# Dense attention: the target-row addition moved from VectorE to GpSimd for four of every five source tiles

## The reference, cut to what matters

```python
e = leaky_relu(es[src] + ed[dst], 0.2)       # es, ed: one score per node and head
m = segment_max(e, dst, num_segments=n)
w = exp(e - m[dst])
den = segment_sum(w, dst, num_segments=n)
out = segment_sum(h[src] * (w / den[dst])[:, :, None], dst, num_segments=n)
```

## Time and profile before

| | |
|---|---|
| median of three runs | 7711.75 us (7710.52 to 7715.44) |
| profiled execution, its own time | 7714.48 us |
| its span, first to last instruction | 7712.8 us |
| VectorE busy in the span | 4335.9 us, 56% |
| TensorE busy | 5320.6 us, 69% |
| ScalarE busy | 2284.1 us, 30% |
| GpSimd busy | 1473.0 us, 19% |
| mean granted TensorE clock | 0.85 |

### The profile page before, as it was taken

The page is one execution under the profiler, slowest core; times in us unless marked ns, Lnnn a source line. Parts: engine busy times, 40 slices in busy tenths (PEclk is TensorE's granted clock), DMA queues, the critical chain, the costliest instruction groups (busy, mean ns, idle before and its releaser), DMA issues. The chain is left out here.

```text
span 7712.8 us, 81237 instructions
## 1 busy us (share of the span) xinstructions
PE 5320.6 (69%) x21589; PEld 3583.0 (46%) x21589; DVE 4335.9 (56%) x6661; ACT 2284.1 (30%) x3965; POOL 1473.0 (19%) x1601
## 2 busy tenths in 40 slices
PE   0223788877888599898597639639925777666976
PEld 0011344443444366677475418538823333335754
DVE  6100599946999322232684460301138999987857
ACT  0000211122111233222363103212215777754611
POOL 0775166602666000001000000030020000000000
PEclk9655899998999699999798869769967888877978
DMA  0011433354334100033230002145523444432200
GB/s 25 26 38 52 188 100 108 99 168 168 110 100 97 43 8 8 10 96 113 87 112 21 1 13 69 36 151 186 182 67 120 155 156 155 149 92 92 91 12 17
DMA packets 379927, 679.26 MB, mean 88 GB/s; under 512 B 94754, under 2 KB 306907, under 8 KB 372156
## 3 DMA queue, kind: packets, MB, share of 16 engines
q1 hardware_dynamic: 304364, 519.11, 20.5%
q0 software_dynamic: 75344, 157.40, 7.9%
HBM read 503.61 MB, written 172.62 MB: 88 GB/s over the span
## 5 line engine op out<-in xcount | busy, mean ns | idle before, releaser
L598 POOL DMA_INDIRECT sum_rows_in<-rel_table,rel_row x880 | 847.8, 963 | 455.1 <-issue 234.5
L622 DVE TENSOR_SCALAR sum_hot_cell<-x_nodes 128x1500 bf16<-128x1500 f16 (+1 forms) x880 | 892.4, 1014 | 1.0 <-issue 0.9
L676 PE MATMUL ps<-sum_hot_cell,sum_hot_src 128*128 128x500 bf16 x2640 | 766.1, 394 | 165.2 <-issue 84.5
L1504 PE MATMUL ps<-att_ring,acc 125*65 125x500 f32 x1000 | 606.8, 693 | 303.8 <-DVE att_ring L1326 303.5
L545 PE MATMUL ps<-rel_diag,rel_xt 128*128 128x512 f32 x800 | 436.1, 693 | 407.7 <-issue 175.7
L681 PE MATMUL ps<-sum_rows_in,sum_hot 128*128 128x256 f32 x1760 | 592.0, 415 | 65.3 <-issue 63.7
L778 PE MATMUL ps<-aux,sum_wide 125*125 125x256 f32 x2500 | 579.1, 387 | 54.5 <-ACT sum_wide L727 54.5
L1512 PE MATMUL ps<-acc,att_ring 125*125 125x257 f32 x2500 | 561.2, 387 | 73.4 <-DVE att_ring L1326 46.0
L942 POOL COPY aux<-prep_xin 128x256 f32 x75 | 30.1, 415 | 2987.4 <-DVE prep_xin L977 2987.4
L1442 ACT ACTIVATE att_ring<-att_ring,att_src 125x625 f32<-125x625 f32 x750 | 545.4, 804 | 126.3 <-DVE att_ring L1307 126.2
L1307 DVE TENSOR_TENSOR att_ring<-att_ring,att_rows 125x3125 f32<-125x3125 f32 (+1 forms) x162 | 512.4, 3169 | 93.8 <-ACT att_ring L1401 92.6
(11 more groups left out here) (432 smaller groups left out, 7532.4 us busy)
## 6 DMA issues: line engine op xcount, KB each, us to landing
att_cell<-cells SPq DMA_DIRECT2D x150, 781.2 KB, 4.7
att_masks<-masks SPq DMA_DIRECT2D x150, 762.9 KB
rel_table<-rel_stage SPq DMA_DIRECT2D x50, 2048.0 KB
ffn_w<-in_L_ffn_W SPq DMA_DIRECT2D x64, 1024.0 KB, 7.3
sum_cell<-cells SPq DMA_DIRECT2D x250, 156.2 KB, 2.2
masks<-sum_stage POOLq DMA_DIRECT2D x25, 762.9 KB, 11.7
sum_rows_in<-rel_table,rel_row POOLq DMA_INDIRECT x880
cells<-x_nodes SPq DMA_DIRECT2D x5, 2031.2 KB
```

The lines of the kernel that those rows point to most:

```text
L598: pool.indirect_dma_start(rows_in[:, b, u, :], None, table, bass.IndirectOffsetOnAxis(rows[:, k:k + 1], 0)).then_inc(gathered[b], 16)
L622: dve.tensor_scalar(hot_cell[:, b, u, :], K.columns[:, :, 0:CW], K.cell[:, k], None, ALU.is_equal).then_inc(s_hot, 1)
L676: pe.matmul(K.ps[:, bass.ds(side * 4 + j, 1), 0:BW].rearrange("p a n -> p (a n)"), hot_src[:, b, u, :], hot_cell[:, b, u, j * BW:(j + 1) * ...
L1504: pe.matmul(K.ps[0:W, side, 0:BAND], node_rows[s][0:NPT, h, :], ring[0:NPT, b % RB, v, 0:BAND], start=s == 0, stop=s == NT - 1).then_inc(s ...
```

## The change

`lower(b)` no longer adds the row to five tiles. VectorE makes only the first tile of a batch (`own_tiles`; all five in batch 0), and it makes it whole, without ScalarE's Relu: one scalar_tensor_tensor of 125x625, max(both + 0.8 s, low row), where `both` is the sum of the two rows. GpSimd adds the low row to the other four tiles, in two instructions of 125x1250 each, and once per group, from the second on, makes `both` (125x625). Two counters are new: `s_low` (GpSimd's pairs, for which the exponentials of tiles 2 to 5 wait) and `s_both`. ScalarE's bend(b) has four Relus, none in batch 0. To make room in memory `top` and `low` move into the tile `K.gate`, which is idle in these stages, and the tiles of the routed expert layer are freed after it.

```diff
--- before.py
+++ after.py
@@ -1218,12 +1218,14 @@
         s_row, s_rowed, s_max, s_top, s_wide, s_rows = (ph.sem(n) for n in ("row", "rowed", "max", "top", "wide", "rows"))
         s_z, s_w, s_e, s_p, s_mm, s_out = (ph.sem(n) for n in ("z", "w", "e", "p", "mm", "out"))
         s_diag, step, s_bias = ph.sem("diag"), ph.sem("step"), ph.sem("bias")
+        s_low, s_both = ph.sem("low"), ph.sem("both")
         ring = ph.sb("ring", [P, RB, UN, GW])
         warm = ph.sb("warm", [P, 1])
         if across:
             s_turned, s_back, turned = ph.sem("turned"), ph.sem("back"), ph.sb("turned", [P, GW])
-        rows = ph.sb("rows", [P, 2, 2, GW])
-        top, low = ph.sb("top", [P, heads, NT]), ph.sb("low", [P, heads, NT])
+        rows, both = ph.sb("rows", [P, 2, 2, GW]), ph.sb("both", [P, GW])
+        idle = K.gate[:, :, :].rearrange("p t e -> p (t e)")
+        top, low = (idle[:, j * 4 * NT:(j * 4 + heads) * NT].rearrange("p (h t) -> p h t", h=heads) for j in range(2))
         src8, src2, dst8 = (ph.sb(n, [P, NT, 4]) for n in ("src8", "src2", "dst8"))
         s_parts = ph.sem("parts")
         bias, total = ph.sb("bias", [P, D]), ph.sb("total", [P, NT, heads])
@@ -1244,6 +1246,18 @@
             return q == g and g * UN < loops
 
         diags = [sum(looped(c) for c in range(b + 1)) for b in range(NB)]
+
+        def own_tiles(b):
+
+            return UN if b == 0 else 1
+
+        def by_vector(batches):
+
+            return batches + UN - 1
+
+        def by_pool(batches):
+
+            return (batches - 1) * 2
 
         @block.sync
         def _(sp):
@@ -1297,15 +1311,21 @@
             def lower(b):
 
                 r = b // UN
-                parts = UN if b == 0 else 1
+                h = r // NG5
                 if b % UN == 0:
                     dve.wait_ge(s_rows, (r + 1) * 2)
-                for i in range(parts):
-                    n = UN // parts
-                    dve.wait_ge(s_z, b * UN + (i + 1) * n)
-                    here = ring[0:NPT, b % RB, i * n:(i + 1) * n, :]
-                    dve.tensor_tensor(here, here, rows[0:NPT, r % 2, 1, :].unsqueeze(1).to_broadcast([NPT, n, GW]),
-                                      ALU.add).then_inc(s_w, n)
+                if b == 0:
+                    dve.wait_ge(s_parts, 3)
+                    link(dve.tensor_tensor(both[0:NPT, :], rows[0:NPT, 0, 0, :], rows[0:NPT, 0, 1, :], ALU.add))
+                elif b % UN == 0:
+                    dve.wait_ge(s_both, r)
+                for u in range(own_tiles(b)):
+                    if b >= RB:
+                        dve.wait_ge(s_mm, ((b - RB) * UN + u + 1) * MM)
+                    t = b % UN * UN + u
+                    dve.scalar_tensor_tensor(out=ring[0:NPT, b % RB, u, :], in0=both[0:NPT, :],
+                                             scalar=src8[0:NPT, t, h:h + 1], in1=rows[0:NPT, r % 2, 1, :],
+                                             op0=ALU.add, op1=ALU.max).then_inc(s_w, 1)
                 if looped(b):
                     dve.wait_ge(s_cell[b % CB3], (b // CB3 + 1) * 16)
                     for u in range(UN):
@@ -1371,6 +1391,21 @@
                     finish(b // UN - (heads - 1) * NG5 - 1)
             finish(NG5 - 1)
 
+        @block.gpsimd
+        def _(pool):
+            pool.wait_ge(s_rows, 2)
+            for b in range(1, NB):
+                r = b // UN
+                row, low_row = (rows[0:NPT, r % 2, j, :] for j in range(2))
+                if b % UN == 0:
+                    pool.wait_ge(s_rows, (r + 1) * 2)
+                    pool.wait_ge(s_w, by_vector(r * UN))
+                    pool.tensor_tensor(both[0:NPT, :], row, low_row, ALU.add).then_inc(s_both, 1)
+                for i in range(2):
+                    pool.wait_ge(s_z, (b - 1) * (UN - 1) + (i + 1) * 2)
+                    here = ring[0:NPT, b % RB, 1 + 2 * i:3 + 2 * i, :]
+                    pool.tensor_tensor(here, here, low_row.unsqueeze(1).to_broadcast([NPT, 2, GW]), ALU.add).then_inc(s_low, 1)
+
         @block.scalar
         def _(act):
 
@@ -1378,7 +1413,8 @@
 
                 act.wait_ge(s_wide, r + 1)
                 if r >= 2:
-                    act.wait_ge(s_w, (r - 1) * UN * UN)
+                    act.wait_ge(s_w, by_vector((r - 1) * UN))
+                    act.wait_ge(s_low, by_pool((r - 1) * UN))
                 act.copy(rows[:, r % 2, :, 0:BAND], K.ps[:, 5:7, 0:BAND]).then_inc(s_rows, 1)
                 act.copy(rows[:, r % 2, :, BAND:GW], K.ps[:, 7, 0:2 * NPT].rearrange("p (j n) -> p j n", j=2)).then_inc(s_rows, 1)
 
@@ -1394,7 +1430,7 @@
                 h = r // NG5
                 if b % UN == 0:
                     act.wait_ge(s_rows, (r + 1) * 2)
-                for u in range(UN):
+                for u in range(own_tiles(b), UN):
                     s = b % UN * UN + u
                     if b >= RB:
                         act.wait_ge(s_mm, ((b - RB) * UN + u + 1) * MM)
@@ -1437,7 +1473,10 @@
                 r, q = b // UN, b % UN
                 h, g = r // NG5, r % NG5
                 for u in range(UN):
-                    act.wait_ge(s_w, b * UN + (u + 1 if b == 0 else UN))
+                    if u < own_tiles(b):
+                        act.wait_ge(s_w, by_vector(b) + 1 if b else u + 1)
+                    else:
+                        act.wait_ge(s_low, by_pool(b) + (u + 1) // 2)
                     here = ring[0:NPT, b % RB, u, :]
                     act.activation(here, here, ACT.Exp, bias=src2[0:NPT, q * UN + u, h:h + 1]).then_inc(s_e, 1)
                 if q == 3 and r + 1 < NGR:
@@ -2459,24 +2498,28 @@
...
-        K.slots, K.slot_gate = sb("slots", [P, 2, NT], I32), sb("slot_gate", [P, 2, NT])
...
+        with ExitStack() as scope:
+            def routed(name, shape, dt=F32):
+                return scope.enter_context(nc.sbuf_tensor(name, shape, dt))
+
+            K.slots, K.slot_gate = routed("slots", [P, 2, NT], I32), routed("slot_gate", [P, 2, NT])
...
```

More of the change, by code:

```diff
@@ L2459, in build @@
         add_mean(K, "res2")
-        K.slots, K.slot_gate = sb("slots", [P, 2, NT], I32), sb("slot_gate", [P, 2, NT])
[L2463 to L2479, removed]
+        with ExitStack() as scope:
+            def routed(name, shape, dt=F32):
+                return scope.enter_context(nc.sbuf_tensor(name, shape, dt))
+            K.slots, K.slot_gate = routed("slots", [P, 2, NT], I32), routed("slot_gate", [P, 2, NT])
+            K.block_expert = routed("block_expert", [P, NB_X], I32)
+            K.sorted_x = nc.dram_tensor("sorted_x", [NB_X * TB + 2 * NPAD, D], F32).ap()
+            K.sorted_y = nc.dram_tensor("sorted_y", [NB_X * TB, D], F32).ap()
+            def load_expert(sp, e, w1, w2, b1, b2, sem):
+                one = bass.ds(e, 1)
+                sp.dma_start(w1, K.inp["L2_ffn_W1"][one, :, :].rearrange("a (c p) n -> p (a c) n", p=P)).then_inc(sem, 16)
+                sp.dma_start(w2, K.inp["L2_ffn_W2"][one, :, :].rearrange("a (c p) n -> p (a c) n", p=P)).then_inc(sem, 16)
+                sp.dma_start(b1, K.inp["L2_ffn_b1"][one, :].rearrange("a (c p) -> p (a c)", p=P)).then_inc(sem, 16)
+                sp.dma_start(b2, K.inp["L2_ffn_b2"][one, :].to_broadcast([P, D])).then_inc(sem, 16)
+            gates, n = top_two_gates(K, "L2_ffn_bg", 8)
+            node_pass(K, "prep2", ["L2_ffn_Wg"], [("L2_ffn_bg", 8)], normed(K), 0, norm=lambda t: K.x[:, t, :],
+                      keep_xn=True, batch_post=gates, batch_steps=n, gate_cols=8)
+            route_tokens(K, "route2")
+            sorted_experts(K, "ffn2", load_expert, ACT.Gelu, 8)
+            combine_experts(K, "join2")
```

## The result

The changed kernel takes 8020.8 us (8015.4 to 8023.4, four runs) where the kernel before takes 7713.6 in the same session: 1.0392 times as long, 95% interval 1.0379 to 1.0405, +307 us. Forecast were 8015 us and +302. The profiled execution spans 8013.7 us. By stage, from the first row preparation to the last result on VectorE: four-head attention 1081.2 to 1324.7 us (+243.5), the one-head ones 364.5 to 397.7 and 369.2 to 395.8 (+33.2, +26.6). Together that is 303 us, as much as the profiled spans differ by (301).

What follows compares the result with a forecast made beforehand. VectorE was taken to bound the four-head stage at 10.2 us per batch; 290 there, +16 in the one-head stages and -4 of startup gave +302, about 8015 us; range 7430 to 8150.

Steps and rivals of the forecast that it cites:

- Taking turns: Likeliest case, 0.56: VectorE's two-tensor passes and GpSimd's additions exclude each other, so their times add; +302 us.
- saving per pair: Overlap of fixed parts when a VectorE and a GpSimd instruction take turns: 0.16 us per pair, taken from copies.
- signs named for the profile: Expected in the trace: L1326 passes drawn out or spaced, additions about 2.8 us, VectorE's and GpSimd's busy shares summing to batch length.
- The sum per batch: Second attention, four heads: 7.6 VectorE + 5.9 GpSimd - 2.2 x 0.16 = 13.1 us against 10.2, +290 us.
- waits that I had costed at nothing: Sum-row wait at new groups costed at nothing; late exponentials of tiles 2 to 5 given about one batch of slack.
- The wait for the sum row: At a new group VectorE waits for GpSimd's sum row: costed at nothing, uncovered some 40 us in all.
- cover: Rows are copied about two VectorE passes, 6.7 us, early, which was to hide the making of the sum row.
- One-head stages: First and third attention: the end at 4114 to 4122 us instead of 4111, about +8 us each, +16.
- the equal start: First attention: batch 18's L1326 starts at about 4041 us after the change, as before, because TensorE's backlog goes.
- The rival that ran freely: VectorE and GpSimd run side by side in every four-head batch, 7.6 us of VectorE longest: -288, about 7425 us; chance 0.22.
- Sharing word by word: One read path serves both engines, 11.7 us per four-head batch: about 7860 us, no change to 7890; chance 0.17.

Runs made afterwards that it cites:

- probe: Kernel before with a stage of 18 pairings of five VectorE and five GpSimd instructions ahead; two-SBUF-tensor additions took 13.95 and 14.39 us alone, 26.6 together.
- e1: Changed kernel with GpSimd's two additions per batch replaced by two memsets each, so it only writes there; 7606.1 us, 0.9871 of the kernel before.
- e2: Changed kernel with each GpSimd addition replaced by a copy of the same tiles onto themselves; 7660.8 us, 0.9942 of the kernel before.
- e5: Kernel before with three GpSimd multiplications of 125x200 added per attention batch, which nobody waits for; 7825.6 us, 1.0131 of the kernel before.
- e3: Changed kernel with the additions to four tiles back on VectorE, GpSimd making only the sum row; 1.0001 of the kernel before.
- v2: v1 without fused tile and sum row except in batch 0, VectorE adding to three tiles from PSUM, GpSimd to two; 0.9974 of the kernel before, another chip.
- v1: Changed kernel with GpSimd adding to two tiles, VectorE's fused pass and two-tile addition reading PSUM rows where available; 1.0004 of the kernel before.
- e6: e1 with each mask transfer after the first three cut to 625 of 3125 columns; 7468.1 us, one run.

## Why the prediction was right, step by step

*Taking turns.* Right, and shown: probe, e1, e2's trace and e5. The saving per pair of 0.16 us, from the copies, was 0.35 for additions. Of the signs named for the profile one was wrong: the busy shares do not add up to the batch's length, but to 814 us in 500, because held time counts as busy.

*The sum per batch.* From batch 1 to 87 the four-head stage takes 12.9 us per batch after (5898.1 to 7009.8 us, 86 steps) and 10.4 before (5864.1 to 6756.2); forecast were 13.1 and 10.2. The nearness hides two errors. The addition was mis-sized: 2.4 us instead of 2.8, so 4.8 + 0.26 for 5.9. (The estimate of 2.75 us from the Trainium skill, GPSIMD Engine Reference, section 3.1, is too high for this addition as well, and fits the probe's, on three separate tiles: 2.81 us.) And with that the sum would be 11.9 to 12.3, by either saving per pair, so 0.6 to 1.0 us per batch are waits that I had costed at nothing. VectorE stood still for 36 of 500 us. From 5860 to 7130 us it waited 44.8 us for exponentials, which come late behind a held fused pass, and 27.7 us ahead of the fused pass at group starts: 0.7 us per batch. How far GpSimd's additions used that time is not measured.

*The wait for the sum row.* I took 6.7 us of cover. In the first attention VectorE stood still for 6.07 us at a group start:

```profile
3855.18 1.29 POOL L1403 TENSOR_TENSOR att_both<-att_rows 125x625 f32<-125x625 f32 x1 [20.24 <-ACT att_rows L1419]
3856.58 0.87 DVE L1326 SCALAR_TENSOR_TENSOR att_ring<-att_both,att_src,att_rows 125x625 f32<-125x625 f32 x1 [6.07 <-issue]
```

Over all groups it is 57.7 us, so the cover did not hold everywhere. In e3, which keeps this wait, a group start costs 1.0 us more than before, about 19 us in the four-head stage, and v2, which has no sum row and no fused tile, is 0.3% faster than v1 by their ratios. So it is a term of some 20 us, not of nothing, and a small part of the 307.

*One-head stages.* Wrong in size: +33 and +27 instead of +8. A line was misread: the L1326 at 4040.5 us is batch 19's (the first batch is 0). Batch 18's started 20 us earlier, so the equal start that the prediction puts down to TensorE's backlog is none:

```profile
4020.68 3.40 DVE L1326 SCALAR_TENSOR_TENSOR att_ring<-att_ring,att_cell 125x3125 f32<-125x3125 f32 x1
```

The forecast end does not hang on it, since it was added up from 4041 us. After the change batch 18's L1346 starts at 4054.1 us, 13 later than worked out, and the end came like this:

```profile
4117.68 3.41 DVE L1346 SCALAR_TENSOR_TENSOR att_ring<-att_ring,att_cell 125x3125 f32<-125x3125 f32 x1
...
4141.52 0.37 ACT L1454 COPY xt_nodes<-ps 125x256 f32<-125x256 f32 x1 [31.34 <-PE ps L1551]
```

I let TensorE follow VectorE by one batch; it followed by two (23.8 us): at the full clock a batch takes it 11.1 us, and it works without a pause from 4094.7 us until its last batch is done, so it still owes the batch before when the last one is ready. The four-head stage erred the other way, +243.5 for +286, and the total came out at 307 for 302. That the point was hit within 6 us is partly luck.

*The rival that ran freely.* It did not happen, but its price was wrong: 7425 us where e1 gives 7606. (Sharing word by word, priced at 7860 and at most 7890, did not happen either; see the probe.) I summed the engines and left out the transfers, which at 10.2 us per batch moved 154 GB/s without being waited for, and which e1's VectorE waited for at 156 GB/s (e1, e6).

## What to carry to other kernels

Before work goes from VectorE to GpSimd, look at operands, not at busy shares: if VectorE's instructions read two SBUF tensors and GpSimd's read SBUF at all, their times add, and a GpSimd addition at 1.9 ns per element against 1.04 loses more than it takes over. In the probe, one VectorE operand in PSUM, or GpSimd work that only writes, left both engines their times beside such passes; VectorE's fp32 copy is the exception, for it reads one tensor and excludes GpSimd's additions, copies and memsets all the same. In a trace, durations of unedited instructions that jump by the other engine's length are the sign, and busy shares then count waiting; and before pricing the gain of an engine set free, add the transfers as one more engine to the sum.

## What was not expected of the hardware

A GpSimd instruction of 0.52 us was held for up to 3.3 us by a VectorE pass (e5), so that it took seven times its length in the median, while VectorE lost only 0.2 us per pass: here the short instruction paid most. A GpSimd memset of 1250 fp32 (1.14 us) costs nearly what its copy does (1.22), but does not touch VectorE's two-tensor passes.
